# A seven-chunk fused convolution and mixture-of-experts kernel: its beginning reordered, and experts, scatters and gathers set to other beats

## The reference

```
xn  = layernorm(x)                                   # over channels, no affine
r   = relu(batchnorm(xn @ w_reduce))                 # 128 -> 32 channels
kg  = r @ w_span + b_span                            # 16 groups x 7 x 7 per pixel
x   = x + sum over 7x7 of kg * patch(xn)             # each pixel has its own kernel, one per group of 8 channels
t   = layernorm(x) as 12544 tokens
p   = softmax(t @ gate_w + gate_b); the two best of 8 experts, weights p
out = x + sum over the two of p_e * (gelu(t @ W1[e] + b1[e]) @ W2[e] + b2[e])
```

## Time and profile before

| | us |
|---|---|
| three runs, median (lowest to highest) | 1255.81 (1252.32 to 1256.5) |
| the profiled execution, its own time | 1253.85 |
| its span, first to last instruction | 1251.9 |
| PE busy | 893.8 (71%) |
| PE weight loads busy | 797.0 (64%) |
| DVE, ACT, POOL busy | 553.2, 518.5, 497.5 (44%, 41%, 40%) |
| mean granted TensorE clock | 0.860 of full |

### The profile page before, as it was taken

One profiled execution on the slowest core, in us unless ns is written; L12 is line 12 of the kernel. 1 busy time (PEld: TensorE's weight loads), 2 busy tenths in 40 slices (PEclk: granted clock), 3 DMA queues, 4 the chain that ended last, 5 costly groups with the idle time before them and its releaser, 6 DMA issues. The chain is left out here.

```text
span 1251.9 us, 30108 instructions
## 1 busy us (share of the span) xinstructions
PE 893.8 (71%) x11249; PEld 797.0 (64%) x11249; DVE 553.2 (44%) x1722; ACT 518.5 (41%) x1246; POOL 497.5 (40%) x538
## 2 busy tenths in 40 slices
PE   1228989849987878877888779878889677435620
PEld 0127878748876878867777678867788566335620
DVE  4112354315453655446464365535564365224322
ACT  3314444434744546453655437444544235212310
POOL 4000010730046730766127650567307560755035
PEclk9997887779988969989899889889889798865775
DMA  5487563626345563637526465444725231223112
GB/s 117 109 181 211 119 137 62 162 55 164 87 111 154 135 156 86 169 95 172 129 69 180 112 154 124 121 131 102 166 54 142 82 86 54 72 84 98 51 46 66
DMA packets 184136, 144.05 MB, mean 115 GB/s; under 512 B 65166, under 2 KB 169614, under 8 KB 183544
## 3 DMA queue, kind: packets, MB, share of 16 engines
q1 hardware_dynamic: 169080, 116.41, 38.1%
q0 software_dynamic: 14336, 25.72, 8.0%
q10 hardware_dynamic: 576, 0.00, 0.0%
HBM read 89.70 MB, written 52.36 MB: 113 GB/s over the span
## 5 line engine op out<-in xcount | busy, mean ns | idle before, releaser
L528 POOL DMA_INDIRECT xrows<-tn,pos x224 | 218.0, 973 | 300.5 <-DVE pos L896 168.3
L1080 PE MATMUL kg<-rT,wk 98*112 98x112 f32 x1792 | 265.4, 312 | 39.6 <-DVE kb L766 30.7
L617 ACT ACTIVATE kb<-kg 112x448 f32<-112x448 f32 x336 | 172.6, 543 | 273.8 <-PE kg L1080 272.0
L543 POOL DMA_INDIRECT got<-yrows,pos x224 | 216.6, 967 | 161.4 <-issue 69.0
L1080 PEld LDWEIGHTS kg<-rT,wk 98*112 98x112 f32 x1792 | 226.9, 200 | 64.1 <-DVE kb L766 32.6
L1115 PE MATMUL e<-kb,win 112*32 112x64 f32 x6272 | 199.5, 291 | 10.9 <-ACT kb L617 9.3
L659 ACT ACTIVATE hT<-h,staged 128x128 f32<-128x128 f32 x420 | 131.6, 366 | 140.4 <-PE h L1182 139.9
L1115 PEld LDWEIGHTS e<-kb,win 112*32 112x32 f32 x6272 | 169.5, 129 | 29.6 <-ACT kb L617 13.3
L1194 PE MATMUL xy<-staged,hT 128*128 128x128 f32 x840 | 140.3, 301 | 46.0 <-ACT hT L659 25.2
L914 DVE COPY staged<-table 128x642 f32 x245 | 125.0, 511 | 99.9 <-DVE yo L923 55.5
L1194 PEld LDWEIGHTS xy<-staged,hT 128*128 128x128 f32 x840 | 112.1, 200 | 67.6 <-ACT hT L659 55.8
(11 more groups left out here) (105 smaller groups left out, 772.2 us busy)
## 6 DMA issues: line engine op xcount, KB each, us to landing
win<-xpad SPq DMA_DIRECT2D x56, 784.0 KB
xin<-xrows SPq DMA_DIRECT2D x56, 256.0 KB
yrows<-yo SPq DMA_DIRECT2D x56, 256.0 KB
xpad<-xs SPq DMA_DIRECT2D x280, 28.0 KB
xs<-in_x_dram SPq DMA_DIRECT2D x56, 112.0 KB
t_row<-in_x_dram SPq DMA_DIRECT2D x56, 112.0 KB
out_dram<-t_row SPq DMA_DIRECT2D x56, 112.0 KB
xrows<-tn SPq DMA_DIRECT2D x4, 896.0 KB, 8.5
```

Of the source, the lines that this page charges most:

```text
L528: pool.indirect_dma_start(xrows[n % 2], bass.IndirectOffsetOnAxis(ap=pos[n % 2][:, i:i + 1], axis=0), tn[:, c * C:(c + 1) * C], None) \
L543: pool.indirect_dma_start(got[:, slot * C:(slot + 1) * C], None, yrows[n % 2], bass.IndirectOffsetOnAxis(ap=pos[n % 2][:, k * COLS + c:k * ...
L617: act.activation(kb[:, lo:lo + 4 * PATCHES], kg_bank[j % 2][0:WIN, 0:4 * PATCHES], ACT.Copy) \
L1080: mm = pe.matmul(kg_bank[j % 2][0:WIN, i * PATCHES:(i + 1) * PATCHES], wk[:, at:at + WIN], r[:, :, :, b4 + i], start=True, stop=True, skip ...
```

## The change

- **Beginning.** Units 2 and 3 are loaded at once, into the third `t_row` tile, which isn't needed until chunk 2. Of each unit 0 to 2 the first 64 channels are written to `xpad` first, then the windows of that half are loaded, then the other half is written. Five of the zero transfers go from ACT's queue, and the six rows take two transfers in place of six. Features alternate between two banks of PSUM. DVE, not POOL, clears two tiles. DVE takes the moments of unit 3 behind its copies of the first kernels.
- **Roots.** `requests_made` is gone, with its wait.
- **Beats.** `START` 33 to 36, scatters 9 to 33, gathers 39 to 57, the chunk's store 62, the next `t_row` 63; the gate's steps one later (58 and 60 become 59 and 61) or one earlier (1 and 3 become 0 and 2), the softmax to ranks one earlier, PE's `rank` 8 to 7, `places` 9 to 8, the first `logits` 62 to 63.

```diff
-    START = 33
-    SCATTER = (10, 32)
-    GATHER = (36, 54)
+    START = 36
+    SCATTER = (9, 33)
+    GATHER = (39, 57)
...
+        def unit_rows(u):
+
+            if u in (2, 3):
+                return t_row[2][:, (u - 2) * 8 * C:(u - 1) * 8 * C]
+            return xs[u % 2][:, :]
...
         def _(sp):
             def load_x(u):
-                if u >= 2:
-                    sp.wait_ge(xt_done, 2 * (u - 1))
-                    sp.wait_ge(xn_out[u % 2], 16 * 28 * (u // 2))
+                if u >= 4:
+                    old = u - 4 if u < 6 else u - 2
+                    sp.wait_ge(xt_done, 2 * (old + 1))
+                    for half in range(2):
+                        xn_written(sp, old, half)
...
             load_x(0)
             load_x(1)
+            sp.dma_start(wred3[:, :].rearrange("p (a d) -> p a d", a=3),
+                         w_reduce.unsqueeze(1).to_broadcast([128, 3, CR])).then_inc(const_loaded, 16)
...
-            sp.wait_ge(pool_const, 1)
-            zero_borders()
-            put_xn(0)
             load_x(2)
-            put_xn(1)
+            load_x(3)
+            sp.wait_ge(zeros_set, 1)
+            zero_borders(sp, 0, (1,))
+            put_xn(0, (0,))
+            put_xn(1, (0,))
             load_window(0, 0, 0)
             load_window(0, 0, 1)
+            put_xn(2, (0,))
+            load_window(0, 0, 2)
+            load_window(0, 0, 3)
+            load_t(0)
             sp.dma_start(gate_sb[:, :], gate_w).then_inc(const_loaded, 16)
             sp.dma_start(gate_bias[:, :], gate_b.partition_broadcast(T)).then_inc(const_loaded, 16)
-            put_xn(2)
-            load_window(0, 0, 2)
-            load_window(0, 0, 3)
-            load_x(3)
-            load_t(0)
+            zero_borders(sp, 1)
+            for u in range(3):
+                put_xn(u, (1,))
...
             def rstd1(u):
-                requests_made()
                 pool.wait_ge(ve1_ready, u + 1)
...
             def rstd2(v):
-                requests_made()
                 pool.wait_ge(ve2_ready, v + 1)
...
-            act.wait_ge(bn_ready, 2)
+            act.wait_ge(zeros_set, 1)
+            zero_borders(act, 0, (0,))
...
-            moments1(3)
             for j in range(16):
                 if on_dve(j):
                     take_kernels(0, j)
+            moments1(3)
```

More of the change, by code:

```diff
@@ L296, in metaformer_kernel, with unit_cols, early_set2, feat_bank @@
         GROUPS = (NT + 3) // 4
+        def unit_rows(u):
+            if u in (2, 3):
+                return t_row[2][:, (u - 2) * 8 * C:(u - 1) * 8 * C]
+            return xs[u % 2][:, :]
+        def unit_cols(u, lo, count):
+            return unit_rows(u)[:, lo * C:(lo + count) * C].rearrange("p (k c) -> p k c", c=C)
+        def early_set2(u):
+            return u in (1, 3)
+        def feat_bank(k):
+            return back if k < 4 and k % 2 else misc
+        def xnT_at(k):
+            return conv[0] if k < 4 and k % 2 else xnT
+        def r_lin_at(k):
+            return conv[1] if k < 4 and k % 2 else r_lin
+        def xn_written(eng, u, half):
+            eng.wait_ge(xn_out[half][u % 4], 16 * 14 * (u // 4 + 1))
+        ZEROS = [8, 6]
+        def zero_borders(eng, half, sides=(0, 1)):
+            if half == 0 and 0 in sides:
+                for row in (0, ROWS - 3):
+                    eng.dma_start(xpad[:, :, row:row + 3, :].rearrange("h j r f -> (h j) r f"),
+                                  zeros[0:28, 0:B * PW * 64].unsqueeze(1).to_broadcast([28, 3, B * PW * 64])) \
+                        .then_inc(zeros_out[0], 16)
+            for side in sides:
+                pw, j0 = ((0, 0), (PW - 1, 11))[side]
+                for j in range(j0, j0 + 3):
+                    to = xpad[half, j, 3:3 + H, :].rearrange("r (b p c) -> r b p c", b=B, p=PW)[:, :, pw, :]
+                    eng.dma_start(to, zeros[0:H, 0:B * 64].rearrange("p (b c) -> p b c", b=B)) \
+                        .then_inc(zeros_out[half], 16)
         @block.sync
@@ L331, in load_window @@
                     if u >= 0:
-                        sp.wait_ge(xn_out[u % 2], 16 * 28 * (u // 2 + 1))
-                if k < 8:
-                    sp.wait_ge(zeros_out, 16 * ZEROS)
+                        xn_written(sp, u, half)
+                if n == 0:
+                    for h in range(half + 1):
+                        sp.wait_ge(zeros_out[h], 16 * ZEROS[h])
                 row = 8 * n + 2 * s
@@ L342, in load_t @@
                     sp.wait_ge(out_stored[n % 3], 16 * 8 * (n // 3))
+                if n == 2:
+                    sp.wait_ge(xt_done, 2 * 4)
+                    for u in (2, 3):
+                        for half in range(2):
+                            xn_written(sp, u, half)
                 for a in range(2):
@@ L372, in store_rows @@
                              yo[k % 2][:, 0:have * C].rearrange("p (i c) -> p i c", c=C)).then_inc(y_stored[k % 2], 16)
[L374 to L385, removed]
             def zero_rows():
@@ L530, in scatter @@
                     .then_inc(scattered, 16)
-                count["scattered"] += 16
             def gather(n, i):
@@ L624, in apply2 @@
                 if n == 0:
-                    act.wait_ge(zeros_out, 16 * 18)
+                    for half in range(2):
+                        act.wait_ge(zeros_out[half], 16 * ZEROS[half])
                     act.wait_ge(rows_zero, 16 * 6)
@@ L1212, in _ @@
             pe.wait_ge(const_loaded, 16)
-            for k in range(4):
-                turn_xn(k)
-                reduce_channels(k)
+            turn_xn(0)
+            turn_xn(1)
+            reduce_channels(0)
+            reduce_channels(1)
+            turn_xn(2)
+            reduce_channels(2)
+            turn_xn(3)
+            reduce_channels(3)
             pe.wait_ge(wk_step, 6)
```

152 lines of the change are left out of this document (84 added, 68 removed).

## The result

The change made the kernel slower by 0.8%: 1261.95 us, median of 12 runs (1254.57 to 1265.28), against 1250.13 for the kernel before (12 runs beside them), a ratio of 1.0083 with a 95% interval of 1.0055 to 1.0111. Forecast were 1201 us and a range of 1177 to 1226. The profiled execution is one of its quickest, at 1254.63 us, and that of the kernel before, 1253.85 us, lies above its own median, so the two traces show little of the loss; what they do show is that nothing was won. A ratio with an interval is that of the runs counted as fast, and for the kernels that spread most (START 35, all mended) these can be the quicker half alone, so the medians of all runs are given beside it there.

What follows compares the result with a forecast made beforehand. PE was taken to set the pace, its waits for expert rows and a DVE copy lengthening chunks; -14 - 39.1 - 5 - 4 + 9 = -53 from 1253.85 us gave 1201 us, range 1177 to 1226.

Steps and rivals of the forecast that it cites:

- The beginning, -14: Chunk 0, beat 27: unit 4 lands at 127.5, not 141.7, gaining 14 us; bounds 5 to 22.
- The wait at START, -39.1: Beat 33, chunks 1 to 6: four more beats for scatters shorten or remove PE's expert-row waits, gaining 39.1 us.
- the work moved is not less: At START: the same work remains, with tiles of the chunk before last now also in beats 33 to 35.
- New waits, +9: `logits` at beat 63, root at beat 34, gathers and `mix` near chunk's end: 9 us lost, 39 at upper ends.
- None is on a shorter path than before: Among the new waits: a gain would need one to shrink, and none has a shorter path; no gain counted.
- The chunk's end, -5: PE's turn of `tn` one beat later meets ready rows: 5 of 6.9 us gained, between nothing and 6.9.
- The tail, -4: After chunk 6's `pos`: three beats' tiles stand behind it, one beat less ahead, gaining 4 us.
- The roots, costed at nothing but 1.4 us: Beat 34 on ACT: root is late next; its 1.4 us landing wait goes; ACT may stand 0 to 2 us.
- The waits move on: Rival: the middle chunks' four waits turn into others, their 24.5 us don't come, 1225 us; chance 0.2.
- The clock gives more: Rival: without START waits PE runs at 2.4 GHz there, 10 us more gained, 1191 us; chance 0.14.
- Slower: Rival: `t_row`, loaded three beats later, lands after beat 6 and holds DVE's addition, `back` and PE; 1260 us, chance 0.03.
- middle chunks at 146 with the `xin` waits gone: Sign against the forecast: chunks 2 to 5 still take 146 us, not 141, though expert-row waits went; another wait grew.

Runs made afterwards that it cites:

- START 35: Changed kernel with START 35 for 36: median 0.982 of the kernel before on a 1256 us chip; 0.9888, 0.9973, 0.9972 on 1560 us chips.
- all mended: Changed kernel with START 35, `places` at 9, unit 4 loaded before tables, unit 3's writes after chunk 0's second-half windows: 1230.93 us, 0.983 by all-run medians.
- the new beginning and old beats: Changed kernel, old beats, unit 4 loaded before tables, unit 3's writes after chunk 0's second-half windows: 0.9865, median 1235.14 us.
- roots held: Changed kernel with every beat set back and `requests_made` put back, so POOL waits before each root: 0.9941 of the kernel before, 1560 us chip.
- the beginning alone: Changed kernel with every beat set back, keeping new beginning and free roots: 0.9912 of the kernel before (1560 us chip), 0.9929 (1256 us chip).

## Why the prediction was wrong, step by step

- **The beginning, -14: right mechanism, mis-sized.** It gave 5.7 us. SP's first window of the second half went out 4.8 us later than worked out, the load of unit 4 was fully issued 5.1 us later (124.06 for 119) and took 9.7 us from there to be used in place of 8.5, and PE waited 36.7 us in place of 25. It came out next to the lower bound given, 5.
- **The wait at START, -39.1: the step that failed.** The waits went: 50.6 us in chunks 1 to 6 became 3.3. But the sum took a wait removed for time gained. Net idle time fell by 31, and PE's busy time rose by as much in this profile and by 39 in the second. The sentence "the work moved is not less" looked only at how much work PE does, not at what now stands between two dependent products.
- **New waits, +9: the other failed step.** I bounded `logits`, the root and the gathers, none of which cost anything visible. Missed were `places` ahead of the copy of beat 9 (20.5 us in place of 5.0) and the `hT` and `xT` waits (40 us more, 35 of them in chunks 1 to 6). "None is on a shorter path than before" was wrong too, the other way: the waits for `cum` and `conv` fell from 31.1 us to 3.3. Both missed waits could be read from what was at hand: the order of DVE's instructions, and 45.2 us of `hT` and `xT` waits in the trace before, which I did not list.
- **The chunk's end, -5: right.** PE waited 1.8 us for `tn` in place of 6.9.
- **The tail, -4: its term was right**, 186.9 in place of 190.2 us from `pos` to the end. The term that was missing is ahead of it: `pos` came 10.5 us later after the last convolution. PE's work there grew by 5.2 us, at a clock of 0.64 in place of 0.77, and the rest is idle. With all mended it takes as long (43.8 us), with the new beginning and old beats 37.2, so some 6 us are the price of the new beats wherever START stands, and the rest comes without them; how the 6 divide between the gate's later steps and the moved tiles was not tried apart.
- **The roots, costed at nothing but 1.4 us:** nothing measurable, as said, though only two 1560 us chips were asked.
- **The rivals.** *The waits move on* named the truth, but I let it eat only the middle chunks' 24.5 us; it ate more than that and the beginning's gain with it. *The clock gives more* had the wrong sign. The Trainium skill (TensorE: Matmul & The Clock Gate, HAM oscillation) has idle gaps bring the engine to half rate; here the trace does not agree: 31 us of idle time were taken out of chunks 1 to 6, five of the six long waits at START with them, and the granted clock went from 0.90 to 0.87. *Slower* had the wrong place: the load of `t_row` was issued by 606.14 and first used at 629.76, with 23.6 us to spare where it had 27.0.

```profile
602.58 3.56 SPq L397 DMA_DIRECT2D t_row<-in_x_dram  x8
...
629.76 0.41 DVE L835 TENSOR_TENSOR t_row<-t_row,back 112x256 f32<-112x256 f32 x1
```

What would have shown it wrong was named: middle chunks at 146 with the `xin` waits gone. Chunk 3 took 147.5. Chunks 2, 4 and 5 took 146.3, 150.3 and 146.4.

## What to carry to other kernels

Before moving a step by a beat, read on each engine what it now stands ahead of, and list the small waits of the same pair of instructions, not only the large ones: 1 to 3 us, tens of times, cost as much here as the seven long ones had. When PE is 80% busy, size the removal of a wait twice, as idle time and as granted clock over the same stretch, since busy time can give back what idle time loses. And when a wait at one step depends on two patterns sliding against each other, time the neighbouring offsets: between 35 and 36 these waits differ by 44 us, more than the 39.1 that the move was to bring. Last, before two kernels are compared by their profiles, look where each profiled run lies among its own: 19 us under the median was nearly all of the gain that two such rows showed.

## What the hardware did unexpectedly

**PE's busy time follows the clock.** Over chunks 1 to 6, busy time by clock is 682.3 x 0.90 = 614, 713.0 x 0.87 = 620, 695.2 x 0.88 = 612, 721.3 x 0.86 = 620, 727.7 x 0.84 = 611: the same work to 1.5%, and the clock is read to two digits. No run settles what lowers the clock at the new beats; all that is shown is that less waiting came with a lower clock, in every profiled variant with START 35 or 36 on the usual chips.

**Three chips took 1560 us for a kernel that takes 1250 on others.** On one of them, PE and POOL at the same time, in the kernel with roots held:

```profile
588.98 0.27 PE L1184 MATMUL e<-kb,win 112*32 112x64 f32 x1 [1.80 <-issue]
```

```profile
588.97 0.95 POOL L573 DMA_INDIRECT xrows<-tn,pos  x1 [0.30 <-issue]
...
412.96 0.94 POOL L573 DMA_INDIRECT xrows<-tn,pos  x1 [0.30 <-issue]
444.74 1.95 POOL L550 TENSOR_TENSOR rs<-ve,minus_half 112x8 f32<-112x8 f32 x1 [30.83 <-issue]
```

The issues take 0.94 us as everywhere. The wait of 30.83 us behind the last one is not for its landing, though the expectation above takes 29 us for that: the root needs `ve` from DVE, and that comes at 444.43, behind DVE's other work on a slower PE. With the roots free, POOL's root waits for `ve` as well, 32.6 us. What does go with the scatters is PE's pace. While they are under way its single products of 0.27 us stand up to 1.8 us apart with nothing named that they wait for, 189 us in all for this line; 6 us after the last is issued (412.96) it runs as usual again:

```profile
444.43 0.17 DVE L800 TENSOR_TENSOR ve<-vi,sq 112x8 f32<-112x8 f32 x1
```

```profile
415.41 0.26 PE L1149 MATMUL kg<-rT,wk 98*112 98x112 f32 x1 [2.54 <-issue]
...
420.81 1.80 PE L1184 MATMUL e<-kb,win 112*32 112x64 f32 x56
```

What makes these chips so was not tried. A ratio from such a chip orders variants at best: START 36 shows there as the worse one too, but all mended (0.992 and 0.9968) can't be told from the beginning alone (0.9912).
